# Short matmuls set one by one between the long ones on TensorE, in an eight-batch LoRA and mixture kernel on one core

## What is computed

```python
# layer 0: one LoRA adapter of rank 16 for each batch, picked by an index
Bx  = einsum('bni,bri->bnr', x, B[adapter_ids])
x   = x + einsum('bnr,bor->bno', Bx, A[adapter_ids])
# layer 1: dense product, and a mixture of 8 rank-16 experts, the best two of each token
base   = einsum('btd,od->bto', x, W)
logits = einsum('btd,ed->bte', x, Wr) + bias of the batch's language
gates  = softmax of the two largest logits, zero for the others
h      = einsum('btd,erd->bter', x, A)
x      = x + base + 2.0 * einsum('bter,bte,eor->bto', h, gates, B)
```

## Time and profile before

| what | value |
|---|---|
| median of 3 runs | 1562.73 us (1558.95 to 1563.44) |
| span of the profiled execution, first to last instruction | 1559.5 us |
| mean granted TensorE clock | 0.996 |
| PE, PEld, DVE, ACT, POOL busy | 99%, 83%, 79%, 46%, 5% |
| matmuls, weight loads | 7430, 7430 |

### The profile page before, as it was taken

One profiled execution on the slowest core, in us unless ns is written; L12 is line 12 of the kernel. 1 busy time (PEld: TensorE's weight loads), 2 busy tenths in 40 slices (PEclk: granted clock), 3 DMA queues, 4 the chain that ended last, 5 costly groups with the idle time before them and its releaser, 6 DMA issues.

```text
span 1559.5 us, 20275 instructions
## 1 busy us (share of the span) xinstructions
PE 1541.5 (99%) x7430; PEld 1298.3 (83%) x7430; DVE 1230.4 (79%) x1692; ACT 714.2 (46%) x911; POOL 79.7 (5%) x119
## 2 busy tenths in 40 slices
PE   9989999999999999999999999999999999999998
PEld 8778878888888888888888888888888888888887
DVE  6998878977799767887688776997769976787665
ACT  6522222544445444455445444454444554445442
POOL 2333331000000000000000000000000000000000
PEclk9999999999999999999999999999999999999999
DMA  9899999787777767687676977667776777666564
GB/s 263 224 276 281 265 254 246 215 230 205 218 231 220 216 196 231 219 229 220 203 224 196 257 207 218 216 205 231 209 218 226 215 217 195 214 219 217 198 219 160
DMA packets 303109, 347.04 MB, mean 223 GB/s; under 512 B 204890, under 2 KB 236682, under 8 KB 302346
## 3 DMA queue, kind: packets, MB, share of 16 engines
q1 hardware_dynamic: 293602, 314.28, 69.8%
q0 software_dynamic: 9136, 30.94, 6.0%
q10 hardware_dynamic: 272, 0.52, 0.1%
HBM read 278.52 MB, written 66.72 MB: 221 GB/s over the span
## 4 chain that ended last, share of the span: by engine, by line
PE 88%; DVE 5%; SPq 4%; DMA 2%; issue 1%; ACT 0%; DVEq 0%; ACTq 0%
PE pb L804 26%; PE pb L805 26%; PE pb L806 26%; PE pb L378 4%; PE pb L380 3%; PE pb L533 2%; SPq L669 2%; SPq L292 2%; DVE raw L684 1%; DVE xl L558 1%; DMA out_dram<-ost 1%; DVE pool_a L540 1%; DMA raw<-in_L_cond_W_dram 0%; DMA an<-in_L_cond_A_dram 0%; PE pb L319 0%
## 5 line engine op out<-in xcount | busy, mean ns | idle before, releaser
L796 ACT CAST wh<-raw 128x1024 fp32r<-128x1024 f32 (+1 forms) x453 | 475.4, 1049 | 705.3 <-PE pb L806 670.9
L800 DVE TENSOR_TENSOR wl<-raw,wh 128x1024 fp32r<-128x1024 f32 (+1 forms) x453 | 552.1, 1219 | 261.3 <-ACT wh L796 260.0
L804 PE MATMUL pb<-wh,sh 128*128 128x512 f32 x1568 | 612.8, 391 | 0.5 <-DVE ost L858 0.5
L805 PE MATMUL pb<-wl,sh 128*128 128x512 f32 x1568 | 611.6, 390 | 0.0
L806 PE MATMUL pb<-wh,sl 128*128 128x512 f32 x1568 | 611.2, 390 | 0.0
L806 PEld LDWEIGHTS pb<-wh,sl 128*128 128x128 f32 x1568 | 294.3, 188 | 62.8
L804 PEld LDWEIGHTS pb<-wh,sh 128*128 128x128 f32 x1568 | 294.5, 188 | 56.2 <-DVE wl L800 0.9
L805 PEld LDWEIGHTS pb<-wl,sh 128*128 128x128 f32 x1568 | 294.6, 188 | 55.1
L378 PE MATMUL pb<-awb,xah 128*128 128x304 f32 x512 | 139.0, 305 | 0.3 <-DVE xal L355 0.3
L380 PE MATMUL pb<-awb,xal 128*128 128x256 f32 x512 | 134.6, 280 | 0.0
L804 PE MATMUL pb<-wh,xh 128*128 128x512 f32 x256 | 101.5, 396 | 0.8 <-DVE xl L558 0.8
(11 more groups left out here) (153 smaller groups left out, 1258.6 us busy)
## 6 DMA issues: line engine op xcount, KB each, us to landing
raw<-t_scr SPq DMA_DIRECT2D x392, 512.0 KB, 4.1
xst<-in_x_dram SPq DMA_DIRECT2D x448, 64.0 KB, 3.8
out_dram<-ost SPq DMA_DIRECT2D x72, 256.0 KB, 3.5
raw<-in_L_cond_W_dram SPq DMA_DIRECT2D x124, 128.0 KB, 5.3
raw<-bt_scr SPq DMA_DIRECT2D x28, 512.0 KB, 3.6
out_dram<-u SPq DMA_DIRECT2D x56, 256.0 KB, 2.9
t_scr<-raw POOLq DMA_DIRECT2D x32, 256.0 KB, 4.4
t_scr<-tst POOLq DMA_DIRECT2D x16, 512.0 KB, 6.7
```

What stands on the lines that cost most here:

```text
L796: e.copy(pair_split(wh, g), pair_source(g)).then_inc(c_wh, 1)
L800: e.tensor_tensor(out=pair_split(wl, g), in0=pair_source(g), in1=pair_split(wh, g).bitcast(f32), op=ALU.subtract).then_inc(c_wl, 1)
L804: e.matmul(o, h, wh[:, g % RING, k, :], start=start, stop=False)
L805: e.matmul(o, h, wl[:, g % RING, k, :], start=False, stop=False)
```

## The change

The helpers and deltas of a slot are cut into single steps. `aux_step(e, n, u, j)` issues the j-th of the eight helper matmuls, `delta_step(e, n, u, k)` the k-th of the two delta matmuls; the waits of the block (`aux_wait`, `delta_wait`) stand ahead of the first step. `products`, `gated_products` and the second half of `first_products` now write out their twelve long matmuls one by one and issue one step after each of the first eight (helpers) or the first two (deltas). The same matmuls are issued, with the same operands. No other engine's program changes. The helpers of batch 0, the one unit of batch 1 that falls in a `first_gated` slot, and the deltas of batches 0 and 1 stay in blocks.

```diff
+        def one_product(e, o, h, l, g, k, part, start, stop):
+            if part == 0:
+                return e.matmul(o, h, wh[:, g % RING, k, :], start=start, stop=False)
+            if part == 1:
+                return e.matmul(o, h, wl[:, g % RING, k, :], start=False, stop=False)
+            return e.matmul(o, l, wh[:, g % RING, k, :], start=False, stop=stop)
...
+        def between(e, n, j, aux, change):
+            if aux is not None and j < 8:
+                aux_step(e, n, aux, j)
+            if change is not None and j < 2:
+                delta_step(e, n, change, j)
...
-        def products(e, b, i):
+        def products(e, b, i, aux=None, change=None):
...
-            for k in range(2):
-                for t in range(2):
-                    toks = slice(t * P, (t + 1) * P)
-                    last = three_products(e, pb[:, 2 * c + t, :], sh[:, h % SR, k, toks], sl[:, h % SR, k, toks], g, k,
-                                          first and k == 0, end and k == 1)
+            for j in range(12):
+                k, t, part = j // 6, j // 3 % 2, j % 3
+                toks = slice(t * P, (t + 1) * P)
+                last = one_product(e, pb[:, 2 * c + t, :], sh[:, h % SR, k, toks], sl[:, h % SR, k, toks], g, k, part,
+                                   first and k == 0, end and k == 1)
+                between(e, b + 1, j, aux, change)
...
-                if 10 <= i < 26:
+                if 10 <= i < 26 and i % 9 == 8:
                     aux_products(e, 1, i - 10)
-                if i % 9 != 8:
-                    first_products(e, i, 1)
+                elif i % 9 != 8:
+                    first_products(e, i, 1, i - 10 if 10 <= i < 26 else None)
...
+                    aux = AUX_AT.get(i) if n < NB else None
+                    change = i - 44 if n < NB and i >= 44 else None
                     if n < NB:
-                        if i in AUX_AT:
-                            aux_products(e, n, AUX_AT[i])
...
-                        if i >= 44:
-                            delta(e, n, i - 44)
                     if is_lora(b, i):
-                        gated_products(e, b, i)
+                        gated_products(e, b, i, aux, change)
                     else:
-                        products(e, b, i)
+                        products(e, b, i, aux, change)
```

More of the change, by code:

```diff
@@ L373, in aux_products, with aux_step @@
             e.wait_ge(c_xl, 16 * n + u + 1)
-            for k in range(2):
-                cols = awb[:, q % 2 * HK + 2 * kp + k, :, :].rearrange("p s n -> p (s n)")
-                for t in range(2):
-                    toks = slice(t * P, (t + 1) * P)
[L378 to L382, removed]
+        def aux_step(e, n, u, j):
+            q, kp = x_unit(u)
+            k, t, low = j // 4, j // 2 % 2, j % 2
+            if j == 0:
+                aux_wait(e, n, u)
+            cols = awb[:, q % 2 * HK + 2 * kp + k, :, :].rearrange("p s n -> p (s n)")
+            toks = slice(t * P, (t + 1) * P)
+            bank = aux_bank(n, u // 8) + t
+            if low:
+                last = e.matmul(pb[:, bank, 0:LOW], x_low(n, u)[:, k, toks], cols[:, 0:LOW],
+                                start=False, stop=u % 8 == 7 and k == 1)
+            else:
+                last = e.matmul(pb[:, bank, 0:2 * AW], x_high(n, u)[:, k, toks], cols[:, 0:2 * AW],
+                                start=u % 8 == 0 and k == 0, stop=False)
+            if j == 7:
+                last.then_inc(c_ax, 1)
+        def aux_products(e, n, u):
+            for j in range(8):
+                aux_step(e, n, u, j)
         def aux_low(e, n, half):
@@ L530, in delta, with delta_step @@
                 e.wait_ge(c_x1, 16 * n + u - 1)
+        def delta_step(e, n, u, k):
+            q, kp = delta_unit(n, u)
+            if k == 0:
+                delta_wait(e, n, u)
+            at = (q % 2 * HK + 2 * kp + k) * P
+            last = e.matmul(pb[:, delta_bank(n, u), k * HT:(k + 1) * HT], a0g[:, at:at + P],
+                            bxt[:, q // 2 * HT:(q // 2 + 1) * HT], start=True, stop=True)
+            if k == 1:
+                last.then_inc(c_dl, 1)
+        def delta(e, n, u):
             for k in range(2):
[L532 to L535, removed]
+                delta_step(e, n, u, k)
         def adapt(e, n, u):
@@ L801, in pair_lo @@
                             op=ALU.subtract).then_inc(c_wl, 1)
+        def one_product(e, o, h, l, g, k, part, start, stop):
[4 more added lines that the diff above has]
+            return e.matmul(o, l, wh[:, g % RING, k, :], start=False, stop=stop)
         def three_products(e, o, h, l, g, k, start, stop):
-            e.matmul(o, h, wh[:, g % RING, k, :], start=start, stop=False)
-            e.matmul(o, h, wl[:, g % RING, k, :], start=False, stop=False)
-            return e.matmul(o, l, wh[:, g % RING, k, :], start=False, stop=stop)
+            for part in range(3):
+                last = one_product(e, o, h, l, g, k, part, start, stop)
+            return last
         def first_bank(c, t):
@@ L832, in first_products @@
                 q = t // 2 * 2 + h
-                last = three_products(e, pb[:, first_bank(c, t), :], xh0[:, k, q, toks], xl0[:, k, q, toks], i, h,
-                                      k == 0 and h == 0, False)
+                for part in range(3):
+                    last = one_product(e, pb[:, first_bank(c, t), :], xh0[:, k, q, toks], xl0[:, k, q, toks], i, h, part,
+                                       k == 0 and h == 0, False)
+                    if aux is not None and 3 * t + part < 8:
+                        aux_step(e, 1, aux, 3 * t + part)
             if h == 1:
```

31 lines of the change are left out of this document (14 added, 17 removed).

## The result

| | before | changed |
|---|---|---|
| median of 22 runs | 1563.47 us (1558.95 to 1569.18) | 1569.41 us (1565.35 to 1574.15) |
| ratio to before, 95% interval | | 1.0038 (1.0029 to 1.0047) |
| span of the profiled execution | 1559.5 us | 1566.2 us |
| batches 1 to 6, from the trace | 1116.45 us | 1122.14 us |

A forecast was written before the change was run, and what follows sets the result against it. TensorE, busy 99% at full clock, was taken to bound the kernel. Helpers +6.2, deltas +1.2, uncovered wait +3.8 and deltas' wait -0.7 gave +10.5 us on a median of 1562.7: 1573.2 us, range 1562 to 1580.

The forecast's parts named there:

- forecast case: Whole kernel: all four parts hold, +10.5 us to 1573.2 us, own range 1570 to 1576; chance 0.5.
- neutral case: Rival: the order of short and long matmuls costs nothing, only the waits count; +3.1, 1565.8 us; chance 0.2.
- Part 1: Helpers in 111 slots: eight returns to long matmuls instead of one, +0.056 us a slot, +6.2 us.
- part 4: Deltas' six waits for adapt, now behind one long matmul, are met almost in time: -0.7 us.
- part 3: Slot 7 of batches 1 to 6: product waits for wl that helpers used to cover, 0.64 us each, +3.8 us.
- What bounds the kernel: TensorE, busy 99% of the span at full clock: any time added to its stream is paid in full.
- eight are 0.096: Mixed helper slots: eight returns from short to long matmuls at 0.012 us each, the price read after delta bursts.
- Today's 0.04: Helper slots of the kernel before: the one return after the block of eight costs 0.04 us a slot.
- Part 2: Deltas in 96 slots: two returns to long matmuls instead of one, 0.0125 us each, +1.2 us.
- Edits at nothing: c_ax raised some 1.8 us later and c_dl 0.45 later, both covered by other waits, at no cost.
- The relief: Rival: short matmuls in a row are bound by issue or loads, spreading relieves it; -6.4, 1556.3 us; chance 0.1.
- Dearer mixing: Rival: several long matmuls per mixed slot are stretched, the upper bounds hold; +16.5, 1579 us; chance 0.15.

The follow-up runs named there:

- e2: Kernel before, with only slot 7's helpers set singly between the long matmuls in batches 1 to 6: 1567.25 us, ratio 1.0022.
- e6: Kernel before, with slot 7's eight helpers, still one block, behind the first long matmul in batches 1 to 6: 1565.74 us, ratio 1.0018.
- e7: Changed kernel, VectorE's second add_s3 moved from slot 4 to 6, add_s2 sums to 8 and 9: 1565.95 us; control, kernel before with these moves: 1563.70 us.
- e3: Changed kernel, with VectorE's two add_s2 sums moved from slots 5 and 6 to 8 and 9: 1569.34 us, ratio 1.0034.
- e4: Changed kernel, batches 1 to 6: slot 7's helpers in a block ahead, other slots' helpers in two groups of four: 1566.20 us, one run.
- e9: Changed kernel, batches 1 to 6: slot 7's helpers in a block ahead, other slots' helpers in four groups of two: 1562.30 us, one run.
- e10: Probe on the kernel before, leaving out, narrowing, restarting or mixing helpers, another variant per batch; no longer computes the layer: 1542.16 us, one run.
- e1: Changed kernel, with slot 7's helpers in a block ahead of the long matmuls again in batches 1 to 6: 1566.48 us, ratio 1.0021.

## Why the prediction was right, point by point

- **The direction** was right; the size was 0.57 of the forecast: of +10.5 us +5.9 came. 1573.2 was forecast and 1569.4 measured, from a kernel before that was 0.8 us slower in 22 runs than in the 3 of the forecast. That lies in the range of 1562 to 1580, but outside the forecast case's own 1570 to 1576, and as near to the neutral case (1565.8) as to the forecast. The range was wide enough to hold three of the cases, so the time alone doesn't bear out the working. Part 1 was too dear and part 4 gave back too little, both toward a slower kernel; what kept the number inside is the width of the range, and part 3 is what the traces bear out.
- **What bounds the kernel** held. A TensorE at 99% paid every nanosecond.
- **Part 3, the uncovered wait** (+3.8): right in place, count and size. The trace shows 6 x 0.61 = 3.7 us, with idle loads of 0.76 us where 0.9 were forecast; e2 gives 3.95 us and e6 3.80 for the six batches, and e7 takes 3.88 away by moving the sum that makes `wl` late. The step of it that "VectorE's work from 661.87 on is back to back" was also what e7 had to be built on, and e3 failed because I didn't read it.
- **Part 1, the helpers** (+6.2): wrong in size and in its reason. In batches 1 to 6 the mixed helper slots cost 12 x 0.027 = 0.33 us in slots 13 to 41, and 0.10 in the other four, 0.43 a batch, 2.6 us in all; with the 15 slots of batch 0 at the same price 3.0. A mixed helper slot takes 3.80 us where 3.84 was forecast. The step that failed is "eight are 0.096": the price of a return after a burst of deltas isn't paid eight times. The long matmuls that stand behind a helper last 0.233 us on average, 0.006 over an undisturbed one, and the helpers themselves are no dearer than in the block, so a mixed slot leaves 0.061 us over its columns, against 0.042 before. e4 and e9 show that the price doesn't go by the number of returns, and the single slots that it is +0.045 in one kind and -0.007 in the other. "Today's 0.04" was a mean of these two kinds too (0.029 and 0.055).
- **Part 2, the deltas** (+1.2): right in the slots where it can be read by itself. A delta slot went from 2.967 to 2.980 us in eleven of the sixteen of a batch; the slots 48 and 49 have the wait in them, and 44, 55 and 56 show 0, +0.006 and -0.018. In the prediction's working the rows as printed give 0.23 / 2 = 0.115 for a 256-column matmul; the 0.117 is that of four in a row, (240.59 - 240.12) / 4.
- **Part 4, the delta's wait** (-0.7): right in direction, too small. The waits shrank as said, from 2.6 to 1.0 us of idle. But in all the slots 43 to 59 of a batch went from 51.01 to 50.91 us, while part 2 adds up to 16 x 0.013 = 0.21; so some 0.3 us a batch came back, 1.8 in all. The term was too small because it counted only the matmul ahead of the wait. The next long one in the kernel before starts here:

```profile
800.18 0.39 PE L804 MATMUL pb<-wh,sh 128*128 128x512 f32 x1
```

From 799.45 to 800.18 are one long matmul and two deltas, 0.73 us for 0.227 + 0.239: TensorE lost 0.27 us at such a wait and not 0.16, as the delta that waited also took 0.22 us to the next start. Six such waits are 1.6 of the 1.8 us; what the rest is isn't shown. The slots 48 and 49 together went from 6.20 to 6.00 us in batch 3.

- **Edits at nothing**: in batches 1 to 6 that held; ScalarE's copies behind the last helper (line 401) have no idle time there. In batch 0 one of them waits for the last helper 4.49 us instead of 2.64, the 1.8 us that the prediction names. The stretch that it lies in isn't longer for it, as said below.
- **The rivals.** The neutral order falls: e7 is slower than its control by 1.6 us in the six batches even with the deltas' gain in it. The relief is refuted by the same. Dearer mixing was nearer to the mechanism, several stretched matmuls and not one, and wrong in size. The Trainium skill, "TensorE: Matmul & The Clock Gate", section "Back-to-back issue gap", gives the gap by the matmul's own columns as that of a matmul by itself, and says of a stream that loads and matmuls set the spacing together; the formula has no term for what stands beside a matmul. This case's traces need one, a small one: the same matmuls with the same columns leave 0.014 us a helper slot in a block and 0.058 mixed (e10, batches 3 and 6).

The terms add up on the traces: 3.7 (wait) + 2.6 (helpers) + 1.2 - 1.8 (deltas) = 5.7 us in the six batches.

The other 1.0 us of the two spans lies ahead of batch 1, and the traces don't show that it is the change's. That stretch ended at 272.3 us in e9 and 280.2 in e3, whose programs are the same there, and its median is the same in the seven programs that mix the helpers of batch 0 (275.9) and the seven that don't (276.0). The 0.4 us of batch 0 above is hidden in this spread. In that stretch VectorE waits for the weights' transfers; timeline of DVE in the changed kernel:

```profile
198.38 1.30 DVE L703 STREAM_TRANSPOSE raw<-raw 128x512 f32<-128x512 f32 x2 [7.27 <-DMA raw<-in_L_cond_W_dram]
```

and the wait in the same place before:

```profile
196.95 1.30 DVE L684 STREAM_TRANSPOSE raw<-raw 128x512 f32<-128x512 f32 x2 [1.70 <-DMA raw<-in_L_cond_W_dram]
```

## What to carry to other kernels

Before work is moved behind another instruction, ask what it covered: a block of short matmuls ahead of a product was 1 us of shelter for an operand that came 0.7 us late in six places, and these six were worth more than all of the reordering in 207. The check is cheap: set the end of each operand's last write beside the first load that reads it, slot by slot, and note the slack that the moved work gives; where a slack is used up, the next slot's is needed too (e1). And TensorE did better here, over all helper slots though not in each, with its short matmuls in few long blocks than spread among the long ones. Read such a price in slots of every kind: slot 15 alone says one thing of a burst's length and slot 19 another.

## What the runs showed of the hardware that I had not expected

- Short matmuls in a row were hardly dearer for their columns than long ones: 256 columns take 0.117 us in a block, with a load of their own in each, and 512 take 0.227.
- A single 304-column and 256-column pair ahead of twelve long matmuls leaves 0.025 us over the columns, eight 256-column ones 0.01 to 0.02 (e10). Four and eight helpers leave 0.045 and 0.029 us in slot 15, 0.011 and 0.056 in slot 19, and so in the other slots of the two kinds: how much depends on the unit too.
- Two groups in a slot cost as much as eight singles on the mean (0.030 and 0.027 us a slot), one group behind the first long matmul nothing.
- The length of a slot mostly repeats from batch to batch within 0.002 us, so a trace tells 0.02 us a slot where 22 timed runs spread over 10 us.
